# A gated cross-attention and feed-forward block on one Trainium2 core: values computed batch by batch, and the prologue's work dealt out anew

## The reference

```python
n = layernorm(x)                                  # x: (2, 1024, 256), context: (2, 77, 256), 8 heads of 64
q, k, v = n @ Wq, context @ Wk, context @ Wv      # in heads
attn = softmax(q @ k.T * 64 ** -0.5) @ v          # for each batch and head
x = x + tanh(g_xattn) * (attn @ Wo + bo)
y = layernorm(x)
h = relu(quant(quant(y) @ quant(w1).T + quant(b1)))      # 1024 hidden units
x = x + tanh(g_ffn) * (quant(h) @ quant(w2).T + quant(b2))
```

## Time and profile before

| What | us |
|---|---|
| median of 3 runs (lowest, highest) | 124.15 (124.11, 124.31) |
| the profiled execution, its own time | 123.75 |
| its span, first to last instruction | 122.0 |
| PE busy, weight loads (PEld) busy | 115.0, 104.9 |
| DVE, POOL, ACT busy | 97.3, 87.3, 77.2 |

### The profile page before, as it was taken

How to read it: one execution, slowest core, us unless ns; L and a number is a source line. 1 busy time by engine, 2 the same in 40 slices (tenths; PEclk the granted TensorE clock), 3 DMA queues, 4 the chain that set the end, 5 groups by cost and what they waited for, 6 DMA issues and landing times.

```text
span 122.0 us, 2891 instructions
## 1 busy us (share of the span) xinstructions
PE 115.0 (94%) x1013; PEld 104.9 (86%) x1013; DVE 97.3 (80%) x219; ACT 77.2 (63%) x168; POOL 87.3 (72%) x160
## 2 busy tenths in 40 slices
PE   7899995999999989999999999999999999999990
PEld 2589974999797989999999999999999997987880
DVE  2009789799999999899999999989797969437981
ACT  4168682968769895995757484848482919347420
POOL 3003757689498989899888949894989495996620
PEclk9999999999999999999999999999999999999999
DMA  2989799300000000000020002000200020020104
GB/s 73 340 236 370 254 371 377 145 0 5 3 0 3 8 0 0 0 0 5 0 86 5 0 0 86 0 3 5 86 0 0 3 91 0 0 86 8 65 21 172
DMA packets 5312, 8.87 MB, mean 73 GB/s; under 512 B 1175, under 2 KB 2226, under 8 KB 5170
## 3 DMA queue, kind: packets, MB, share of 16 engines
q1 hardware_dynamic: 5210, 8.61, 19.9%
q10 hardware_dynamic: 88, 0.08, 0.2%
HBM read 6.59 MB, written 2.10 MB: 71 GB/s over the span
## 4 chain that ended last, share of the span: by engine, by line
PE 61%; DVE 17%; ACT 8%; POOL 4%; issue 4%; DMA 3%; SPq 0%; ACTq 0%; DVEq 0%; POOLq 0%
PE of_ps L815 18%; PE sc_ps L782 13%; PE h_ps L842 9%; PE of_ps L857 7%; PE tr_ps L794 5%; DVE probs L573 3%; DMA wk_sb<-in_L_xattn_Wk_dram 3%; DVE mx L568 3%; DVE den L580 2%; ACT probs L403 2%; PE tr_ps L718 2%; ACT pT L430 2%; PE tr_ps L764 2%; DVE pT L609 1%; PE tr_ps L857 1%
## 5 line engine op out<-in xcount | busy, mean ns | idle before, releaser
L815 PE MATMUL of_ps<-u_sb,pT 128*128 128x256 f32 x240 | 31.1, 281 | 0.9 <-ACT x2T L450 0.8
L782 PE MATMUL sc_ps<-a_sb,xT 128*128 128x308 f32 x192 | 31.2, 311 | 0.7 <-DVE probs L573 0.7
L815 PEld LDWEIGHTS of_ps<-u_sb,pT 128*128 128x128 f32 x240 | 29.5, 188 | 1.9 <-issue 1.9
L403 ACT ACTIVATE probs<-probs,rstd 128x616 f32<-128x616 f32 x16 | 13.1, 816 | 26.1 <-DVE probs L573 25.8
L782 PEld LDWEIGHTS sc_ps<-a_sb,xT 128*128 128x128 f32 x192 | 27.5, 189 | 1.5 <-issue 1.3
L444 ACT ACTIVATE hid_q<-h_ps,b1z 128x256 int8<-128x256 f32 x58 | 24.7, 491 | 3.9 <-PE h_ps L842 3.9
L282 POOL TENSOR_TENSOR probs<-probs,rden 128x616 f32<-128x616 f32 x16 | 19.5, 1221 | 1.5 <-DVE rden L583 1.5
L331 POOL CAST hid<-hid_q 128x512 bf16<-128x512 int8 x27 | 15.8, 611 | 2.0 <-ACT hid_q L444 2.0
L842 PE MATMUL h_ps<-x2T,w1T 128*128 128x256 bf16 x128 | 16.6, 273 | 0.0
L568 DVE TENSOR_REDUCE mx<-sc_ps 128x8 f32<-128x616 f32 x16 | 12.6, 790 | 4.2 <-PE sc_ps L782 4.2
L842 PEld LDWEIGHTS h_ps<-x2T,w1T 128*128 128x128 bf16 x128 | 12.4, 98 | 1.6 <-ACT x2T L450 0.3
(11 more groups left out here) (113 smaller groups left out, 176.9 us busy)
## 6 DMA issues: line engine op xcount, KB each, us to landing
w_sb<-in_L_ffn_w_dram SPq DMA_DIRECT2D x2, 1024.0 KB, 11.1
out_dram<-x_sb SPq DMA_DIRECT2D x7, 256.0 KB, 2.5
x_sb<-in_x_dram SPq DMA_DIRECT2D x4, 256.0 KB, 8.1
x_sb<-in_x_dram SPq DMA_DIRECT2D x1, 1024.0 KB, 10.0
wk_sb<-in_L_xattn_Wk_dram SPq DMA_DIRECT2D x1, 512.0 KB, 4.0
wq_sb<-in_L_xattn_Wq_dram SPq DMA_DIRECT2D x1, 512.0 KB, 5.0
wv_sb<-in_L_xattn_Wv_dram SPq DMA_DIRECT2D x1, 512.0 KB, 7.8
wo_sb<-in_L_xattn_Wo_dram SPq DMA_DIRECT2D x1, 512.0 KB, 8.8
```

Of the source, the lines that this page charges most:

```text
L403: nc.scalar.activation(probs_v(T), probs_v(T), ACT.Exp, scale=rstd1[:, T:T + 1]).then_inc(exp_done, 1)
L782: ins = nc.tensor.matmul(sc_ps[:, a, 0:HALF], xT[:, T % 2, p, c, :], a_sb[:, q, T // TB, c, HALF * a:HALF * a + HALF], start=first, stop=last)
L815: ins = nc.tensor.matmul(attn_ps, pT[:, T % 2, p, P * c:P * c + P], u_sb[:, q, MC * (T // TB) + c, :], start=first, stop=last)
```

## The change

1. **Values batch by batch.** `valuesT(n)` takes the place of `keysT` for V: n = 0 is batch 0's head pairs 0 and 1, n = 1 its pairs 2 and 3 (both where `keysT` stood), n = 2 all four pairs of batch 1, placed after `scores(1)` and behind a wait for VectorE's low part of the first piece of U, whose bank it overwrites. Each matmul has 77 columns in place of 154, and there are 16 in place of 8. ScalarE copies three times (`v_copy`); the third stands ahead of `exponentials(1)`.
2. **One low part of U on GpSimd.** Piece 1 of batch 0's U is copied whole by ScalarE (`u_copy_whole(0, 1)`) and its low part is taken by GpSimd between `bias_rows` and `softmax_scale(1)`, no longer by VectorE.
3. **VectorE's prologue.** It copies keys 2 and 3 (`kT`, ScalarE's before); the statistics of tiles 4 and 5 stand behind `center(1)`, no longer behind `center(0)`.
4. **ScalarE.** The copy of the first two tiles' transposed rows is two copies of 256 columns, each with a signal; `xT_copy(2)` stands ahead of `exponentials(0)`; `minus_centred(4)` moves to slot 0. In slots 2 to 5 `rowsT_second` stands directly behind `xT_copy`, ahead of `minus_centred` and `hidden_round`.
5. **GpSimd.** `rstd_first(4, 6)` moves from the prologue to slot 1; `hidden_bias` and `output_bias` move from before `softmax_scale(1)` to behind it.

```diff
-        v_banks = of_ps[:, 1, 0:2 * MP], tr_ps[:, 0:2 * MP]
+        v_banks = of_ps[:, 1, 0:MP], tr_ps[:, 0:MP], h_ps[:, 0, 0:HALF]
+        v_pairs = (0, 0, (0, 1)), (0, 2, (2, 3)), (1, 0, (0, 1, 2, 3))
...
             rstd_first(2, 4)
-            rstd_first(4, 6)
             softmax_scale(0)
             bias_rows()
-            hidden_bias()
-            output_bias()
+            u_low(0, 1)
...
                 if s == 0:
+                    hidden_bias()
+                    output_bias()
                     a1_parts(1)
-                if s % 2 == 1 and 3 <= s < TILES - 4:
+                if s % 2 == 1 and s < TILES - 4:
                     rstd_first(s + 3, s + 5)
...
+            def v_copy(n):
+                act.wait_ge(v_psum, n + 1)
+                if n == 0:
+                    act.wait_ge(vz_zero, 1)
+                nc.scalar.copy(values_of(n), values_psum(n)).then_inc(v_ready, 1)
...
+            xT_copy(2)
             exponentials(0)
-            xT_copy(2)
             u_copy(0, 0)
             u_copy(0, 1)
+            u_copy_whole(0, 1)
             u_copy(0, 2)
-            minus_centred(4)
             act.wait_ge(g_in, 32)
             nc.scalar.activation(tg[:, :], g_sb[:, :], ACT.Tanh).then_inc(tg_ready, 1)
+            v_copy(2)
...
+                if 2 <= s < 6:
+                    rowsT_second(s - 2)
-                if live(s + 4) and s > 0:
+                if live(s + 4):
                     minus_centred(s + 4)
...
-                if s >= 2:
+                if s >= 6:
                     rowsT_second(s - 2)
...
+            dve.wait_ge(k_psum, 2)
+            nc.vector.tensor_copy(kT[:, 2:4, :].rearrange("p c m -> p (c m)"), tr_ps[:, 512:512 + 2 * MP]).then_inc(k23_ready, 1)
...
             center(0)
-            stats_first(4, 6)
             rowsT_low(2)
             denominators(0)
             u_low(0, 0)
-            u_low(0, 1)
             center(1)
             u_low(0, 2)
+            stats_first(4, 6)
...
+            def valuesT(n):
+                b, first, pairs = v_pairs[n]
+                for j in pairs:
+                    at = M * (j - first)
+                    for c in range(DK):
+                        ins = nc.tensor.matmul(v_banks[n][:, at:at + M], wv_sb[:, c, P * j:P * j + P],
+                                               ctxT[:, c, M * b:M * b + M], start=(c == 0), stop=(c == DK - 1))
+                ins.then_inc(v_psum, 1)
...
-            keysT(wv_sb, v_psum, (0, 1), v_banks[0])
+            valuesT(0)
...
-            keysT(wv_sb, v_psum, (2, 3), v_banks[1])
+            valuesT(1)
             rowsT(2)
...
             output_weights(0)
             scores(1)
+            pe.wait_ge(u_ready, 1)
+            valuesT(2)
```

More of the change, by code:

```diff
@@ L304, in a1_parts, with u_low @@
                                         ALU.subtract).then_inc(a1_low, 1)
[L306 to L310, removed]
+            def u_low(b, n):
+                pool.wait_ge(u_high, 3 * b + n + 1)
+                pool.wait_ge(u_copied, 1 if b == 0 else 2 + n)
+                nc.gpsimd.tensor_tensor(u_of(b, n, 1), u_whole[:, n, :], u_of(b, n, 0).bitcast(F32),
+                                        ALU.subtract).then_inc(u_low_pool, 1)
             def bias_rows():
@@ L368, in _ @@
                 if s == 0:
+                    hidden_bias()
+                    output_bias()
                     a1_parts(1)
-                if s % 2 == 1 and 3 <= s < TILES - 4:
+                if s % 2 == 1 and s < TILES - 4:
                     rstd_first(s + 3, s + 5)
                 if s in (2, 3):
-                    u_low(s - 2)
+                    u_low(1, s - 2)
                 if s == 5:
@@ L475, in _ @@
             nc.scalar.copy(ctxT[:, :, :].rearrange("p c n -> p (c n)"), sc_ps[:, 0, 0:DK * MP]).then_inc(ctxT_ready, 1)
[L476 to L479, removed]
+            act.wait_ge(k_psum, 1)
+            nc.scalar.copy(kT[:, 0:2, :].rearrange("p c m -> p (c m)"), tr_ps[:, 0:2 * MP]).then_inc(k01_ready, 1)
             for j in range(2):
@@ L489, in _ @@
             a_copy(3)
-            act.wait_ge(xT_psum, 2)
-            nc.scalar.copy(xT[:, :, 0, :, :].rearrange("p i c n -> p i (c n)"),
-                           of_ps[:, 0, :].rearrange("p (i n) -> p i n", i=2)).then_inc(xT_high, 2)
+            for T in range(2):
+                act.wait_ge(xT_psum, 2)
+                nc.scalar.copy(xT[:, T, 0, :, :].rearrange("p c n -> p (c n)"), of_ps[:, 0, D * T:D * T + D]).then_inc(xT_high, 1)
             a1_copy(2)
             a1_copy(3)
-            act.wait_ge(vz_zero, 1)
-            act.wait_ge(v_psum, 1)
-            nc.scalar.copy(values_of(0), values_psum(0)).then_inc(v01_ready, 1)
+            v_copy(0)
             minus_centred(2)
             minus_centred(3)
-            act.wait_ge(v_psum, 2)
-            nc.scalar.copy(values_of(1), values_psum(1)).then_inc(v23_ready, 1)
+            v_copy(1)
+            xT_copy(2)
             exponentials(0)
-            xT_copy(2)
             u_copy(0, 0)
             u_copy(0, 1)
+            u_copy_whole(0, 1)
             u_copy(0, 2)
-            minus_centred(4)
             act.wait_ge(g_in, 32)
             nc.scalar.activation(tg[:, :], g_sb[:, :], ACT.Tanh).then_inc(tg_ready, 1)
+            v_copy(2)
             for s in range(TILES):
@@ L911, in _ @@
                 pe.wait_ge(wqT_ready, j + 1)
-                pe.wait_ge(k_ready, j + 1)
+                if j == 0:
+                    pe.wait_ge(k01_ready, 1)
+                else:
+                    pe.wait_ge(k23_ready, 1)
                 for c in range(DK):
```

46 lines of the change are left out of this document (25 added, 21 removed).

## The result

| What | before | changed |
|---|---|---|
| median, us (20 runs each; lowest, highest) | 123.69 (123.37, 124.31) | 124.39 (124.00, 126.78) |
| ratio to the kernel before, 95% interval | | 1.0047 (1.0030 to 1.0063) |
| span of the profiled execution | 122.0 | 122.8 |
| PE, PEld busy | 115.0, 104.9 | 115.9, 106.3 |
| DVE, POOL, ACT busy | 97.3, 87.3, 77.2 | 97.5, 88.7, 77.8 |

The change makes the kernel slower by about 0.58 us (0.0047 × 123.69; the interval gives 0.37 to 0.78). More runs of the kernel before put its median at 123.69, not at the 124.15 that three runs had given; so the predicted 124.44 lies beside the measured 124.39, but the predicted step, 0.29, is half of the one measured.

A forecast was written before the change was run, and what follows sets the result against it. Bound by VectorE through slot 3 and TensorE from slot 5; GpSimd's 0.77 delay brings slot 5 to 47.24 against 46.95, 0.29 later: 124.15 to 124.44 us. Own range 124.25 to 124.65; with rivals 123.65 to 124.9.

The forecast's parts named there:

- The price of a pass: Value matmuls on TensorE: one pass of 77 columns takes 0.11 us, with ends at 0.066 and 0.13.
- The first rival: Value passes on TensorE: columns set the pace, 0.066 us a pass, `probsT(5)` 0.44 earlier, 123.7 us; chance 0.28.
- the second with its 0.13: Value passes on TensorE hardly shrink, 0.13 us each; kernel 0.86 later, 125.0 us; chance 0.15.
- VectorE's prologue, `scores(0)` and `scores(1)`: Before slot 1: `scores(0)` at 12.42, 0.11 earlier; `scores(1)` at 16.85, 0.28 earlier; `center(1)` at 18.86, 0.92 earlier.
- `exponentials(1)` behind the third copy of values: ScalarE: the copy ends at 21.03, holding `exponentials(1)` until then; gain 0.46 in place of 0.92.
- GpSimd's stretch: From `softmax_scale(1)` to `normalise_second(0)`: 3.47 plus 1.41 for the biases, from 23.07 to 27.95, 0.77 later than 27.18.
- No slack from there to slot 5: From `normalise_second(0)` over `attend(2)` and tile 2's residual to `softmax_scale(5)`: the 0.77 delay stays whole.
- The third rival: GpSimd's delay is eaten up on the way; kernel 0.1 earlier, 124.05 us; chance 0.12.
- The waits for `x2T`: TensorE ahead of `attend(3)` and `attend(4)`: waits of 0.26 and 0.36 us both go.
- GpSimd is late next: At slot 5: `probsT(5)` waits for GpSimd's `softmax_scale(5)` until 47.24; TensorE would be there at 47.1 at the latest.
- `rstd_first(4, 6)` in slot 1 at nothing: GpSimd behind `softmax_scale(2)`: its 1.0 us is covered by idle time of over a microsecond.
- The sum: At slot 5 on TensorE: 47.24 - 46.95 = 0.29 later, solid to the end; median from 124.15 to 124.44.

The follow-up runs named there:

- biases back: The changed kernel with GpSimd's four bias instructions ahead of `softmax_scale(1)` again, behind U's low part; 123.05 us, ratio 0.992 to the kernel before.

## Why the prediction was right and wrong

- **The price of a pass: right.** I took 0.11 between 0.066 and 0.13. Measured on the changed kernel: (12.62 - 11.81)/8 = 0.101 for the first eight passes, (20.66 - 18.83)/16 = 0.114 for the sixteen. The first rival, by which the columns set the pace at 0.066 a pass, is out, and so is the second with its 0.13: with half the columns the passes stayed at 0.107 to 0.109. That the weight load sets the pace was an inference from two durations; the runs fit it and don't prove it, since none changed the width of a load alone. That a pass costs 0.1 whatever it loads is unlikely: the 48 passes of `output_weights(0)` in the kernel before, with loads of 32 columns on 64 rows, take (17.13 - 15.67)/48 = 0.030 each. The formula N/2.4 + 2.5 ns of the Trainium skill (page "TensorE: Matmul & The Clock Gate", section "Back-to-back issue gap") doesn't agree with the trace: counted as 76 cycles, 38 columns would be an estimate of 34 ns, and 107 to 109 were measured. The same page, section "LDWEIGHTS (loading the stationary operand)", puts a load at its columns divided by 1.2, so an estimate of 107 ns for 128: the spacings measured here, 101 to 114 ns, lie around it, though the load's own row lasts 192 ns, since the next one starts before it ends.
- **VectorE's prologue, `scores(0)` and `scores(1)`: right to 0.11.** Counted back to the clock of the kernel before (0.27 less): `scores(0)` at 12.35 for 12.42 forecast, `scores(1)` at 16.74 for 16.85, `center(1)` at 18.76 for 18.86.
- **`exponentials(1)` behind the third copy of values: right, and 0.13 quicker.** Forecast 21.03, measured 21.17 - 0.27 = 20.90. TensorE did not wait for U's low part before `valuesT(2)`; I had it wait until 18.72, and it began at 18.56. `softmax_scale(1)` came at 22.93 for 23.07.
- **GpSimd's stretch: the mis-sized term.** "`normalise_second(0)` starts at 23.07 + 3.47 + 1.41 = 27.95". The stretch without the biases is 3.55, not 3.47 (biases back): of the 0.18 idle time that I took off, 0.08 or so is there whether VectorE is late or not. The four biases cost 5.23 - 3.55 = 1.68, not 1.41: I had measured them from the first start to the last end, 1.45, and taken 0.04 off for an overlap at its ends. There is none: there is a gap ahead of the block (24.42 to 24.51) and one behind it (25.96 to 26.02), and the overlap of 0.05 that `softmax_scale(1)` and the cast had side by side is lost. That makes 1.65 of the 1.68. Together 0.35 too little, against 0.14 too much at `softmax_scale(1)`: `normalise_second(0)` was 0.98 later instead of 0.77.
- **No slack from there to slot 5: right.** The 0.98 are there unchanged at the residual of tile 2 (37.37 - 11.81 = 25.56, against 36.12 - 11.54 = 24.58) and at `softmax_scale(5)` (46.45 - 11.81 = 34.64, against 33.66). The third rival, delay eaten up on the way, is out.
- **The waits for `x2T`: right** in both places. That GpSimd is late next was right too: 0.49 us of waiting at `probsT(5)`.
- **`rstd_first(4, 6)` in slot 1 at nothing: right.** The idle time of over a microsecond behind `softmax_scale(2)` is filled, and `normalise_second(1)` is 0.74 later, less than the 0.98 around it.
- **The sum.** 0.98 instead of 0.77, less the 0.47 by which GpSimd had been ahead of TensorE at slot 5 (0.48 in my sum), is 0.51 instead of 0.29. Measured: 0.58, with 0.37 to 0.78 as its interval. My own range of 124.25 to 124.65 stood for a step of 0.1 to 0.5; it was drawn from the price of a pass alone and gave the 3.47 + 1.41 no width. That the absolute time came out well, 124.44 for 124.39, was luck: three runs had put the kernel before 0.46 above its later median, and that made up for a step that was too small. From 123.69 the same sum gives 123.98.

## What to carry to other kernels

Before moving small work "behind" an instruction, ask what the engine did in its old place: if it filled a wait, it cost nothing there, and on the far side its full price, start to next start and not the sum of its durations, goes onto whatever the in-order queue holds next. Take that price from a place where the block stands between two busy neighbours, and give it a width of its own. When several parts are moved together, look for the one that masks another: here, by the traces, the copy on ScalarE hid what VectorE had gained.

## What the runs showed of the hardware

**The granted clock fell in the one run with very narrow passes.** In the kernel with 38 and 39 columns the granted clock of TensorE was 1.00 up to 24 us, then half (columns: stretch, its length, busy time of PE, PEld, DVE, ACT and POOL with their counts, granted clock, share and rate of the DMA):

```profile
23.00:24.00 1.00, 1.00 (x11) 1.00 (x11) 0.31 (x3) 0.03 (x1) 0.00 (x0) 1.00 0.26 98
24.00:25.00 1.00, 1.00 (x8) 1.00 (x7) 0.00 (x0) 1.00 (x2) 0.00 (x0) 0.60 0.01 4
25.00:26.00 1.00, 1.00 (x6) 1.00 (x6) 0.80 (x1) 0.96 (x4) 0.00 (x0) 0.50 0.00 0
26.00:27.00 1.00, 1.00 (x6) 1.00 (x5) 0.98 (x3) 1.00 (x3) 0.69 (x1) 0.50 0.00 0
```

0.50 is the lower of the two levels, 1.2 GHz. Ahead of it TensorE had done the thirty-two narrow passes without a gap, busy all the time by the profile, with a pass of 38 or 39 columns every 0.109 us. The scores of tile 2, which fell into it, took 27.82 - 24.75 = 3.07 us where those of tile 1 had taken 20.27 - 18.47 = 1.80. The time lost by it was hidden: the passes of `valuesT(2)` are over 23.76 - 11.48 = 12.28 us behind the start of the values, 3.43 later than in the change (20.66 - 11.81 = 8.85), and at `probsT(5)` it is still 3.43 (39.35 against 35.92). So it is the passes that cost this kernel its time. From 27 to 28 us the granted clock was 0.69, from 28 on 1.00.

The profiled execution of the change, with half as many passes of twice the columns, kept 1.00 all along. But another of its twenty executions, of 125.19 us, has a mean granted clock of 0.951. So the clock can fall without the narrower passes, and one run can't say whether they brought it on.

**Four small instructions of GpSimd cost more than their durations.** Where one needs the result of the one before, there is a gap: b1q ends at 24.72 and b1z starts at 24.80, b2q ends at 25.37 and b_gated starts at 25.48. Of those that don't, some overlap by 0.05 us (b2q starts at 24.96, before b1z ends at 25.01; the same with `softmax_scale(1)` and the cast behind it in the kernel before), and some leave a gap all the same (`softmax_scale(1)` to b1q, 24.42 to 24.51). What decides between these was not tried. The four, of 1.31 us of busy time, hold the engine for 1.68.
